# Decoder block on one core: the self-attention values product called once per head pair instead of once per quad, a ring of 14 exponentials, and new order tables for all engines

## The reference

```python
x = x + self_attention(layernorm(x))      # 16 heads, key width 16, value width 64
x = x + cross_attention(ctx, ctx, layernorm(x))   # 64 context rows, feature map exp(z), exp(-z)
x = x + ffn(layernorm(x))                 # out = sigmoid(xr Wr) * (relu(xk Wk)^2 Wv)

# self-attention; the softmax runs over the QUERIES, so each key has its own sum
sim  = einsum('bnkh,bmhk->bnhm', q, k)
attn = softmax(sim / sqrt(16), axis=1)    # axis 1 = n, the queries
o    = einsum('bnhm,bmhv->bnhv', attn, v)
out  = einsum('bnhv,dhv->bnd', o, output_proj)
```

## Time and profile before

| | |
|---|---|
| median of 3 runs | 479.99 us |
| the profiled execution's own time | 479.61 us |
| its span, first to last instruction | 477.8 us |
| TensorE busy | 445.1 us (93%) |
| VectorE busy | 379.9 us (79%) |
| ScalarE busy | 299.0 us (63%) |
| GpSimd busy | 134.5 us (28%) |
| mean granted TensorE clock | 0.982 |
| `weigh` (L653), 512 records | 124.5 us busy |
| `scores` (L639), 256 records | 50.6 us busy |

### The profile page before, as it was taken

How to read it: one execution, slowest core, us unless ns; L and a number is a source line. 1 busy time by engine, 2 the same in 40 slices (tenths; PEclk the granted TensorE clock), 3 DMA queues, 4 the chain that set the end, 5 groups by cost and what they waited for, 6 DMA issues and landing times.

```text
span 477.8 us, 7930 instructions
## 1 busy us (share of the span) xinstructions
PE 445.1 (93%) x2588; PEld 276.3 (58%) x2588; DVE 379.9 (79%) x689; ACT 299.0 (63%) x732; POOL 134.5 (28%) x181
## 2 busy tenths in 40 slices
PE   7779979999999999999999999999999999896985
PEld 3553426535655676557565675566556664485774
DVE  6567676786999988886999989777999787669664
ACT  4348866577688756565796856655796668323431
POOL 2511113113623351214431442114332413142410
PEclk9979999999999999999999999999999999897999
DMA  7852210133221001323301301333102000000001
GB/s 257 309 173 108 78 68 18 45 110 123 101 86 59 12 1 34 114 68 119 105 26 47 105 6 45 113 116 118 59 16 77 36 2 0 23 0 23 2 1 44
DMA packets 20013, 34.02 MB, mean 71 GB/s; under 512 B 2308, under 2 KB 6660, under 8 KB 19844
## 3 DMA queue, kind: packets, MB, share of 16 engines
q1 hardware_dynamic: 19972, 33.52, 21.5%
HBM read 23.02 MB, written 10.49 MB: 70 GB/s over the span
## 4 chain that ended last, share of the span: by engine, by line
PE 75%; DVE 9%; issue 5%; ACT 5%; DMA 3%; POOL 1%; SPq 0%; ACTq 0%; DVEq 0%; POOLq 0%
PE av_bank L653 18%; PE m_bank L591 9%; PE m_bank L593 7%; PE m_bank L592 7%; PE s_pair L639 7%; ACT e_sb L862 4%; DVE nmax L1060 3%; PE m_bank L782 3%; PE m_bank L831 3%; DMA q_parts<-qkt_lo 3%; PE m_bank L795 3%; PE m_bank L770 2%; PE m_bank L820 2%; PE av_bank L603 2%; PE m_bank L670 2%
## 5 line engine op out<-in xcount | busy, mean ns | idle before, releaser
L862 ACT ACTIVATE e_sb<-s_pair,nmax 128x512 f32<-128x512 f32 x256 | 172.8, 690 | 55.9 <-DVE nmax L1060 55.9
L1060 DVE TENSOR_REDUCE nmax<-s_pair 128x2 f32<-128x1024 f32 x128 | 152.9, 1214 | 20.2 <-PE s_pair L639 19.3
L653 PE MATMUL av_bank<-e_sb,v_sb 128*64 128x512 f32 x512 | 124.5, 607 | 4.5 <-POOL v_sb L1330 2.4
L1330 POOL TENSOR_TENSOR v_sb<-v_sb,rsum 128x256 f32<-128x256 f32 x64 | 39.6, 619 | 179.3 <-DVE rsum L1068 169.5
L653 PEld LDWEIGHTS av_bank<-e_sb,v_sb 128*64 128x64 f32 x512 | 31.6, 136 | 57.8 <-issue 46.6
L639 PE MATMUL s_pair<-q_st,k_st 64*128 64x512 f32 x256 | 50.6, 457 | 9.5 <-issue 6.8
L862 ACT ACTIVATION_READ_ACCUMULATOR e_sb<-s_pair,nmax 128x1 f32 x256 | 53.4, 208 | 0.0
L639 PEld LDWEIGHTS s_pair<-q_st,k_st 64*128 64x128 f32 x256 | 21.2, 186 | 55.3 <-issue 35.0
L1357 POOL TENSOR_TENSOR sx<-sx,xrec 128x512 f32<-128x512 f32 x24 | 24.8, 1043 | 46.4 <-DVE xrec L1240 46.4
L591 PE MATMUL m_bank<-wo_hi,ot_hi 128*128 128x256 f32 x120 | 34.9, 291 | 0.0
L593 PE MATMUL m_bank<-wo_lo,ot_hi 128*128 128x256 f32 x120 | 33.5, 279 | 0.0
(11 more groups left out here) (179 smaller groups left out, 857.9 us busy)
## 6 DMA issues: line engine op xcount, KB each, us to landing
q_st<-q_parts SPq DMA_DIRECT2D x31, 256.0 KB, 7.7
k_st<-k_parts SPq DMA_DIRECT2D x62, 128.0 KB
q_parts<-qkt_hi SPq DMA_DIRECT2D x8, 256.0 KB
q_parts<-qkt_lo SPq DMA_DIRECT2D x8, 256.0 KB
out<-x_sb SPq DMA_DIRECT2D x8, 256.0 KB, 2.1
k_parts<-qkt_hi SPq DMA_DIRECT2D x7, 256.0 KB, 2.5
k_parts<-qkt_lo SPq DMA_DIRECT2D x7, 256.0 KB, 5.9
x_sb<-in_x SPq DMA_DIRECT2D x3, 512.0 KB, 9.1
```

The source lines that it names most:

```text
L653: mm = pe.matmul(av_bank[n % AV_BANKS][64 * par:64 * par + 64, :], v_sb[:, m, 2 * p + par, :], e_sb[:, (4 * q + 2 * i + par) % E_RING, :], ...
L862: act.activation(e_sb[:, g % E_RING, :], s_pair[k // 2][:, k % 2, :], ACT.Exp, bias=nmax[:, g % 8:g % 8 + 1], accum_out=esum[:, q % 4, k:k ...
L1060: dve.tensor_reduce(nmax[:, at:at + 2], s_pair[i][:, :, :], AX_X, ALU.max, negate=True)\
L1330: pool.tensor_tensor(v_sb[:, m:m + 2, 2 * p:2 * p + 2, :], v_sb[:, m:m + 2, 2 * p:2 * p + 2, :], rsum[:, q % 4, :].rearrange("p (m h) -> p ...
```

## The change

It does four things.

1. `weigh` is called once per head pair. It takes the four key tiles in a row, and waits for `scale` of the first quad before tile 0 and of the second before tile 2. Its place in TensorE's order is that of the second of the two old calls: behind `scores(2n+2)`, ahead of `scores(2n+3)`.
2. `E_RING` goes from 12 to 14.
3. `feat` moves from the slots around -190 to 61 on VectorE and 68 on ScalarE; `cut("o")` moves from -195 to 10 and -9.
4. All other slots have new numbers: the order of the units changes on every engine, and SyncE's loads as well (`load("rest")`, 1.4 MB, now stands behind the first `qk` writes and ahead of `ld(1)`, `load("o")` comes first).

```diff
-E_RING = 12
+E_RING = 14
...
-    ("cut", ("o",), dict(act=-195, pool=-202)),
-    ("feat", (), dict(dve=-190, act=-192)),
-    ("kf", (0,), dict(pe=57, act=73)),
+    ("cut", ("o",), dict(act=10, pool=-9)),
+    ("feat", (), dict(sp=61, dve=61, act=68)),
+    ("kf", (0,), dict(pe=133, act=155)),
...
-ATTENTION = dict(scores=12, weigh=42, max=(11, 12), exp=(17, 17, 18, 18), rsum=27, scale=22, ot_hi=39, ot_lo=44)
+ATTENTION = dict(scores=14, weigh=41, max=(9, 10), exp=(16, 18, 19, 19), rsum=25, scale=-39, ot_hi=40, ot_lo=42)
...
     for q in range(QUADS):
         at, a = 16 * q, ATTENTION
-        out["pe"] += [(at + a["scores"], "scores", 0, (q,)), (at + a["weigh"], "weigh", 0, (q,))]
+        out["pe"].append((at + a["scores"], "scores", 0, (q,)))
...
         if q % 2:
+            out["pe"].append((at + a["weigh"], "weigh", 0, (q // 2,)))
             out["act"].append((at + a["ot_hi"], "ot_hi", 0, (q // 2,)))
...
-            def weigh(_, q):
-                n, p = q // 2, (q // 2) % NP
-                if q % 2 == 0 and n >= AV_BANKS:
+            def weigh(_, n):
+
+                p = n % NP
+                if n >= AV_BANKS:
 
                     pe.wait_ge(ot_ready, n - AV_BANKS + 1)
-
-                pe.wait_ge(v_scaled, q + 1)
-                for i in range(2):
-                    m = 2 * (q % 2) + i
+                for m in range(NT):
+                    if m % 2 == 0:
+                        pe.wait_ge(v_scaled, 2 * n + m // 2 + 1)
                     for par in range(2):
                         mm = pe.matmul(av_bank[n % AV_BANKS][64 * par:64 * par + 64, :], v_sb[:, m, 2 * p + par, :],
-                                       e_sb[:, (4 * q + 2 * i + par) % E_RING, :], start=(m == 0), stop=(m == NT - 1))
+                                       e_sb[:, (8 * n + 2 * m + par) % E_RING, :], start=(m == 0), stop=(m == NT - 1))
                     mm.then_inc(av_done, 1)
```

More of the change, by code:

```diff
@@ L93 @@
[L93 to L103, removed]
@@ L218 @@
-    ("cut", ("v1",), dict(act=-312, pool=-311)),
-    ("ld", (1,), dict(sp=-111)),
-    ("load", ("o",), dict(sp=-1334)),
-    ("ld", (2,), dict(sp=17)),
-    ("load", ("x1",), dict(sp=-1)),
-    ("load", ("fc",), dict(sp=-355)),
-    ("load", ("rest",), dict(sp=-2172)),
-    ("load", ("feat",), dict(sp=-822)),
-    ("v", (0, 0), dict(pe=27, act=24)),
-    ("v", (0, 1), dict(pe=14, dve=23)),
-    ("v", (0, 2), dict(pe=-5, act=-24)),
-    ("v", (0, 3), dict(pe=15, dve=31)),
+    ("warm", (0, 2), dict(pe=-1503)),
@@ new lines @@
+    ("warm", (1, 2), dict(pe=-311)),
+    ("warm", (2, 2), dict(pe=-1857)),
+    ("ln1", (0,), dict(dve=-1840, pool=-1843, do=-1797)),
+    ("ln1", (1,), dict(dve=-1798, pool=-1779, do=-1797)),
+    ("cut", ("first",), dict(act=-972, dve=-974)),
+    ("cut", ("qk",), dict(act=-1607, dve=-1623)),
+    ("t1", (0,), dict(dve=-1704, pe=-1340, act=-1708)),
+    ("t1", (1,), dict(pe=-326, act=-863, dve=-1621)),
+    ("first", (0,), dict(pe=-157, act=-209, dve=-155)),
+    ("first", (1,), dict(pe=-65, act=-105, dve=-105)),
@@ new lines @@
+    ("qk", (0, 0), dict(dve=-316, sp=-396, pe=-206, act=-316)),
+    ("qk", (0, 1), dict(pe=-204, act=-290, dve=-266, sp=-359)),
+    ("cut", ("v0",), dict(act=-856, dve=-858)),
+    ("cut", ("v1",), dict(act=-338, pool=-317)),
+    ("ld", (1,), dict(sp=-215)),
+    ("load", ("o",), dict(sp=-1794)),
+    ("ld", (2,), dict(sp=-209)),
+    ("load", ("x1",), dict(sp=-1187)),
+    ("load", ("fc",), dict(sp=-346)),
+    ("load", ("rest",), dict(sp=-318)),
+    ("load", ("feat",), dict(sp=-413)),
+    ("v", (0, 0), dict(pe=25, act=19)),
@@ L242 @@
-    ("warm", (7, 1), dict(pe=1530)),
-    ("warm", (8, 1), dict(pe=1811)),
+    ("cut", ("o",), dict(act=10, pool=-9)),
+    ("cut", ("fc",), dict(act=168, pool=173)),
+    ("feat", (), dict(sp=61, dve=61, act=68)),
+    ("kf", (0,), dict(pe=133, act=155)),
+    ("kf", (1,), dict(pe=171, act=170)),
+    ("warm", (3, 1), dict(pe=2402)),
+    ("warm", (4, 1), dict(pe=2199)),
+    ("warm", (5, 1), dict(pe=2367)),
+    ("warm", (6, 1), dict(pe=1485)),
+    ("warm", (7, 1), dict(pe=1958)),
+    ("warm", (8, 1), dict(pe=1987)),
```

330 lines of the change are left out of this document (162 added, 168 removed).

## The result

The changed kernel takes 487.22 us (median of four runs, 485.80 to 489.05) against 480.06 (479.38 to 481.40) for the kernel before, run beside it: ratio 1.0148, 95% interval 1.0102 to 1.0194. It is slower by 1.5%; 471.5 us was forecast, with a range of 463 to 479. The profiled execution took 485.80 us, with a span of 484.0.

The account below looks back on a forecast made before the run. TensorE bounds about 100 to 400 us; early, it waits for a loop through other engines. Terms -6.3 - 1.9 + 4.2 - 5.4 + 4 - 2 - 1 = -8.4 from 479.6 gave 471.2, stated as 471.5 us; range 463 to 479.

Parts of the forecast that it names:

- The start: Before the first scores: with feature steps moved behind them, they start at 20.4 instead of 26.74 us, -6.3 us.
- the clock term: After the first scores: without the pause, matmuls up to 30.61 us no longer run at the lower clock, -1.9 us.
- the first stacked loads come late: Rival at the start: `ld(1)` behind `load("rest")` gives back up to 5 us, 476.5 us in all; chance 0.12.
- the key wait from DRAM: Sign against the forecast, early: a first pair that waits for `k_st` from DRAM would make it wrong.
- the waits for exponentials of over 12 us: Sign against the forecast: TensorE's waits for exponentials summing to over 12 us would make it wrong.
- The early loop: Quads 0 to 13: both product halves wait for the pair's second `scale`, 9.8 us a pair; +4.2 us, 0 to 8.
- The full stretch: Quads 13 to 58, where TensorE fills its windows: -5.4 us for shapes, +4 for spacing, about 287 us.
- the gaps: Quads 13 to 58: uneven spacing of scores makes TensorE wait for exponentials; +4 us, ends -2 and +10.6.
- the -5.4 for shapes: Quads 13 to 58: 34 fewer tile shape changes between neighbouring TensorE units, at 0.16 us each.
- short gaps cost their full price: Rival on spacing between scores: +10.6 us instead of +4, 478 us in all; chance 0.18.
- The end: Last product's first half needs only `scale(62)`: -2 us; cross-attention of the last sequence: -1 us.
- The clock rival: Early loop: TensorE's pauses of over 1 us a pair drop the clock to 1.2 GHz, 486 us; chance 0.05.

Follow-up runs that it names:

- run 10: Changed kernel with each stacked key load written as four copies of 32 rows instead of two of 2 x 32 rows: 478.72 us, ratio 0.996.
- run 9: Changed kernel with `ld(2)` moved on the SyncE queue back behind `qk(1,0)`'s writes: 484.43 us, ratio 1.0072.
- run 1: Changed kernel with `load("rest")` moved on the SyncE queue from ahead of `ld(1)` to behind `ld(3)`: 483.18 us, ratio 1.0059.
- run 13: Changed kernel with four copies a key load and the loads `x1`, `fc` and `rest` behind `ld(4)`: 476.05 us, ratio 0.9858.
- run 14: Changed kernel with four copies a key load, `x1`, `fc`, `rest` behind `ld(4)`, first `qk(1,1)` steps behind quad 2's exponentials: 474.98 us, ratio 0.9857.
- runs 5: Kernel before with feature steps, `kf(0)` and `cut("o")` moved as in the change, `x1` and `fc` behind `ld(4)`: 475.28 us, ratio 0.9896.
- run 15: Kernel before with late feature steps, `x1` and `fc` behind `ld(4)`, four copies a key load, first `qk(1,1)` steps moved later: 474.99 us, ratio 0.986.
- runs 11 and 12: Four copies a key load: in the kernel before, 480.33 us; in the kernel before with late feature steps and `x1`, `fc` behind `ld(4)`, 473.43 us.
- run 7: Changed kernel with `x1`, `fc` and `rest` loaded later and `qk(1,1)`'s ScalarE and VectorE steps behind quad 2's exponentials: 482.84 us, ratio 1.0059.

## Why the prediction was wrong, step by step

**The start, right in itself.** -6.3 was forecast, -6.6 measured (26.74 to 20.18); the clock term held up to 28 us and was lost behind the next pause.

**The step that failed** is the cost of the moved loads. It stands in the forecast's sum at nothing; the forecast had it only as the rival "the first stacked loads come late", with a chance of 0.12 and "up to 5 us". The mechanism was right, the size wrong: `scores(3)` at 44.6 in place of 34.7, 9.9 us. Two things were missing. First, I priced the 1.4 MB at 308 GB/s as if all traffic were alike, and didn't ask how many DMA engines each copy uses. A stacked key load moves at 50 GB/s and holds up what stands behind it. The Trainium skill gives the reason ("DMA: Bandwidth & Descriptors", "Why a DMA increments its semaphore by 16 and not by 1"): the number of engines is the largest up to 16 that divides the slowest dimension (of a size over 1) of both sides, and for copies that SyncE issues they are the lowest-numbered ones. By that rule a slowest dimension of 2 gives two engines, the same two each time; the trace agrees with its share of 0.13, and run 10 with what splitting gave. Second, I costed one move in SyncE's order and not the other, `ld(2)` ahead of `qk(1,0)`'s writes (run 9: 6 us of ScalarE's wait), and so missed who waits for those writes: ScalarE, in front of the exponentials. The start of `scores(2)` shows both causes side by side: 34.2 as it is, 30.7 with `rest` behind (run 1), 30.8 with the four copies (run 10), 29.1 with the loads behind and four copies (run 13). Of the signs named beforehand, the key wait from DRAM came (6.29 us), the waits for exponentials of over 12 us did not (7.9).

**The early loop, nearly right.** From `scores(3)` to 9 it takes 28.6 us (forecast 29.4; run 14 28.8), to 13 52.5 (forecast 53.3).

**The full stretch, half right.** 292.2 us from quad 13 to 58, forecast 287, before 288.5; by its own sign (over 291) the gaps cost more than I took. The merged product costs what I took: 352 of its records take 79.1 us start to start, 3.60 a call, against 1.88 for an old one (360 records, 84.6 us). That is 0.16 a pair, 3.6 us of the -5.4 for shapes; the rest lies with other units, and no run prices it by itself. Taking the -5.4 as it stands, the gaps come to 9.1 us, near my upper end of 10.6 and not to the 4 I chose. Summed start to start, the records of `scores` cost 4.5 us more than before, those of `pt` 2.2, and 2.8 are the wait before `scores(16)`, again a key load. In run 14, without that wait, the stretch takes 289.1 us, gaps of 6. What I had not counted: the stretch now holds 22 pairs' products where it held 45 old calls, so one old call, 1.9 us, has moved behind `scores(58)`, and the gaps are that much dearer still (11.0, and 7.9 in run 14). The rival "short gaps cost their full price" is the nearer one.

**The end, right:** from `scores(63)` on 70.2 us against 72.9, forecast -3 in all. But the last product starts at 418.39 where I had said at least 10 us earlier than 411.9: it inherits the lateness. In run 14 it starts at 408.21, 3.7 us earlier, so that sign was set too high as well.

**The sum.** (479.99 less 8.4 is 471.6; the 471.5 is 0.1 too low.) Against the forecast's 471.2 the profiled run has +9.9 to `scores(3)`, -0.8 to 13, +5.1 to 58 and about +0.4 behind: 485.8. Where the load causes are taken away (run 14, profiled 475.8) the forecast is missed by 4.6: 1.1 to `scores(3)`, 0.9 to 13, 2.1 to 58, the rest behind it.

**The clock rival came true in part.** Its 486 us lies next to the measured 487.2 by luck, since it had no late load in it. In the changed kernel the clock fell behind the new 6.3 us pause. But in runs 10, 13 and 14, where no wait is over 3.1 us, windows of the early loop stand at 0.86 too (24 to 48 us in 13 and 14), while the two-call kernels of runs 5 and 15 show 1.00 there; runs 11 and 12 have 0.86 once (60 to 72 us and 36 to 48). By the executions of run 13 it cost about 5 us, not the 15 of the rival.

```profile
24.00:36.00 12.00, 10.34 (x39) 4.28 (x39) 6.49 (x10) 8.58 (x25) 6.22 (x4) 0.86 0.34 98
36.00:48.00 12.00, 9.80 (x38) 4.11 (x37) 8.36 (x13) 7.17 (x19) 1.28 (x3) 0.86 0.43 133
```

The windows above are run 14's; run 15 has 1.00 in both:

```profile
24.00:36.00 12.00, 10.62 (x45) 5.05 (x44) 8.61 (x11) 9.08 (x23) 5.79 (x3) 1.00 0.60 176
36.00:48.00 12.00, 9.54 (x40) 4.00 (x38) 7.60 (x14) 8.45 (x25) 1.40 (x3) 1.00 0.25 83
```

The run with the most time at full clock shows the stake: one execution of run 13's kernel took 471.33 us at a mean clock of 0.992, the other three 475.8 to 476.7 at 0.978. What tips an execution one way or the other stays open.

## What to carry to other kernels

Before a load is moved, list the whole queue it moves in, and for each transfer how many DMA engines it uses; a copy on few engines is a bottleneck that the size of a load doesn't show, and here it cost nothing until the start got faster. A wait of one engine on a DMA is paid by all that stands behind it in that engine's order. And call structure and a tuned order are one thing: here changing either alone cost 40 and 61 us, which said nothing about the worth of the two together.

## What the runs showed that was not expected

- The form of a copy decides its speed: 2 x 32 rows of 2 KB move at 50 GB/s at a share of 0.13, the same bytes as copies of 32 rows land after a median of 2.3 us.
- Slow copies delay others behind them: the query loads' median fell from 8.3 to 3.1 us when the key loads were split.
- Nearly the same pause before `scores(16)` left the clock at 1.00 in the changed kernel's profiled run (2.75 us; the product behind it took 3.65) and was followed by the lower level in run 7 (2.84 us; 6.17). Executions of run 9's kernel go from 480.24 us at a mean clock of 0.985 to 487.41 at 0.964: 1.5%, more than most of the effects told here.
